# An expert stage with its maxima spread over the turn, its stacks copied by VectorE and its opening's loads in another order

## The reference

```python
def _expert(x, Wqkv, bqkv, Wo, bo, g1, be1, W1, bf1, W2, bf2, g2, be2):   # D=128, H=8 heads of 16, F=512
    qkv = x @ Wqkv.T + bqkv
    q, k, v = jnp.split(qkv, 3, axis=-1)
    q, k, v = (to_heads(q), to_heads(k), to_heads(v))
    attn = jax.nn.softmax(jnp.einsum('bhqd,bhkd->bhqk', q * scale, k), axis=-1)
    ctx = jnp.einsum('bhqk,bhkd->bhqd', attn, v).transpose(0, 2, 1, 3).reshape(b, s, d)
    ctx = ctx @ Wo.T + bo
    x = _layernorm(x + ctx, g1, be1)
    h = jax.nn.gelu(x @ W1.T + bf1, approximate=False)
    h = jax.nn.gelu(h @ W2.T + bf2, approximate=False)
    return _layernorm(x + h, g2, be2)
...
gated = probs * mask            # mask: the two largest of the softmax over 8 experts
gated = gated / (gated.sum(-1, keepdims=True) + 1e-09)
eo = jax.vmap(_expert, ...)(x, Wqkv, ...)
return jnp.einsum('ebsd,bse->bsd', eo, gated)
```

## Time and profile before

| | |
|---|---|
| median of 3 runs | 3488.11 us (3484.39 to 3490.66) |
| the profiled execution: own time, span | 3486.16 us, 3484.2 us |
| busy: PE, DVE, ACT, POOL | 81%, 50%, 56%, 16% |
| mean granted clock of TensorE | 0.91 of full speed |
| DMA | 304.09 MB, mean 87 GB/s |

### The profile page before, as it was taken

One profiled execution on the slowest core, in us unless ns is written; L12 is line 12 of the kernel. 1 busy time (PEld: TensorE's weight loads), 2 busy tenths in 40 slices (PEclk: granted clock), 3 DMA queues, 4 the chain that ended last, 5 costly groups with the idle time before them and its releaser, 6 DMA issues.

```text
span 3484.2 us, 66887 instructions
## 1 busy us (share of the span) xinstructions
PE 2811.9 (81%) x24695; PEld 1992.3 (57%) x24695; DVE 1737.3 (50%) x4806; ACT 1954.3 (56%) x4370; POOL 549.5 (16%) x732
## 2 busy tenths in 40 slices
PE   6778765888887888788887883778888969887898
PEld 5456443666665666566555561355565656555676
DVE  4665663555555555555555542234435453444454
ACT  2233223777776777677666664748435734773443
POOL 2000003333234322433212112000000000000000
PEclk9887876999999999999999986889979989998998
DMA  5000017565465655565445421010000000000000
GB/s 195 0 28 10 1 41 249 150 200 166 155 193 183 207 177 177 166 202 160 144 150 150 136 84 54 1 41 1 1 13 10 1 13 5 1 1 13 5 1 5
DMA packets 162579, 304.09 MB, mean 87 GB/s; under 512 B 19841, under 2 KB 121338, under 8 KB 154554
## 3 DMA queue, kind: packets, MB, share of 16 engines
q1 hardware_dynamic: 158930, 293.69, 27.0%
q0 software_dynamic: 3328, 6.14, 0.6%
HBM read 227.00 MB, written 72.75 MB: 86 GB/s over the span
## 4 chain that ended last, share of the span: by engine, by line
PE 48%; DVE 16%; ACT 11%; issue 11%; DVEq 5%; POOLq 3%; POOL 2%; PEld 1%; DMA 1%; SPq 1%; PEldq 1%; ACTq 0%
PE ps L1515 5%; PE ps L1832 5%; PE ps L1476 4%; PE ps L1497 3%; DVE peaks L2640 3%; PE ps L1313 3%; PE ps L1964 2%; PE ps L1764 2%; PE ps L1540 2%; ACT pt L2143 2%; PE ps L1902 2%; PE ps L1926 2%; PE ps L1549 2%; DVEq L2643 1%; PE ps L1298 1%
## 5 line engine op out<-in xcount | busy, mean ns | idle before, releaser
L2640 DVE TENSOR_REDUCE peaks<-ps 128x1 f32<-128x748 f32 x608 | 555.8, 933 | 557.5 <-PE ps L1476 548.4
L2143 ACT ACTIVATE pt<-ps 128x384 f32<-128x384 f32 x1216 | 570.9, 495 | 241.5 <-PE ps L1497 225.5
L1497 PE MATMUL ps<-qst,kst 98*128 98x128 bf16 x3648 | 403.0, 225 | 30.3 <-ACT pt L2143 10.1
L1497 PEld LDWEIGHTS ps<-qst,kst 98*128 98x128 bf16 x3648 | 271.9, 100 | 192.9 <-ACT pt L2143 62.2
L1133 POOL TENSOR_TENSOR rstd<-var,minus_half 128x6 f32<-128x6 f32 x40 | 53.0, 1324 | 1725.7 <-DVE var L2887 1278.9
L1476 PE MATMUL ps<-kst,qst 96*128 96x374 bf16 x1216 | 311.8, 339 | 11.0 <-DVE peaks L2640 11.0
L1515 PE MATMUL ps<-pt,vst 128*32 128x128 f32 (+1 forms) x7296 | 284.3, 287 | 0.0
L1515 PEld LDWEIGHTS ps<-pt,vst 128*32 128x32 f32 (+1 forms) x7296 | 199.5, 114 | 52.2 <-issue 26.0
L1484 PE MATMUL ps<-identb,peaks 128*2 128x128 bf16 x608 | 60.9, 225 | 82.6 <-DVE peaks L2646 66.6
L2163 ACT ACTIVATE qst<-ps 2x512 bf16<-2x512 f32 x152 | 89.7, 590 | 58.6 <-PE ps L1484 56.3
L1476 PEld LDWEIGHTS ps<-kst,qst 96*128 96x128 bf16 x1216 | 99.9, 102 | 22.7 <-DVE peaks L2640 19.2
(11 more groups left out here) (653 smaller groups left out, 6628.4 us busy)
## 6 DMA issues: line engine op xcount, KB each, us to landing
kst<-saved_k SPq DMA_DIRECT2D x76, 1176.0 KB
wf<-in_l SPq DMA_DIRECT2D x76, 512.0 KB, 5.6
saved_k<-kparts SPq DMA_DIRECT2D x168, 192.0 KB
vst<-saved_v SPq DMA_DIRECT2D x76, 408.0 KB, 4.9
saved_v<-vprod SPq DMA_DIRECT2D x32, 408.0 KB, 2.6
rows<-in_l_rows SPq DMA_DIRECT2D x76, 128.0 KB, 6.4
slots_x<-zeros SPq DMA_DIRECT2D x4, 1216.0 KB, 11.2
wq<-in_l SPq DMA_DIRECT2D x76, 64.0 KB, 4.1
```

What stands on the lines that cost most here:

```text
L1497: mm = pe.matmul(out[:, c * P:(c + 1) * P], kst[0:STACK + SHIFT, m % 3, head, j * P:(j + 1) * P], qst[0:STACK + SHIFT, m % 3, head, :], st ...
L2143: act.activation(pt[:, u % (2 * GROUP), :], entry()[:, 0:H0], ACT.Exp, scale=float(HD) ** -0.5)\
L2640: v.tensor_reduce(peaks[:, g, head:head + 1], entry()[:, :, 0:T // 2], XY, ALU.max)\
```

## The change

- Peaks stand at places 0, 2, 4 and so on to 14 instead of 0, 1, 3, 4, 6, 8, 10, 11. In burst turns the last four stay at place 9.
- The shift of group 0 moves from place 7 to 10, that of group 1 from place 14 of the turn before to place 4 of the tile's own turn.
- `query` moves from place 2 to 3, `out` from 10 to 11, `norm1` from 13 to 14, `turn_x1` from place 15 of turn n+1 to place 1 of turn n+2.
- `stack` becomes one step at place 7: eight products into a pair of banks and one VectorE copy of 96x1024, instead of two steps at 7 and 8 on the ring with ScalarE's copies.
- The opening loads `xb` first, then the key and value weights of all eight experts in one DMA into the room of `wf`, then the tables. `rank` (TensorE's part of the routing) comes before the keys instead of behind the second expert's. GpSimd splits the keys of three experts instead of four. The x tiles 0 to 2 are loaded at the end of the opening; the first burst's `wf` and rows at place 7 of turn 0.
- The semaphore `k_saved` becomes two, one for even and one for odd experts.

The diff:

```diff
@@ -233,7 +233,7 @@
-POOL_SPLITS = 4
+POOL_SPLITS = 3
@@ -274,20 +274,17 @@
 def opening_steps():
...
+    yield "load_xb", 0
+    yield "load_wkv_all",
...
-    yield "load_xb", 0
...
-    yield "load_wkv", 0, 0
+    yield "rank",
...
-        if e + 1 < E:
-            yield "load_wkv", 0, e + 1
...
-        if e == 1:
-            yield "rank",
@@ -295,9 +292,8 @@
-    yield "load_x", 0
-    yield "load_ffn", 0
-    yield "load_rows", 0
+    for m in range(3):
+        yield "load_x", m
@@ -309,30 +305,29 @@
-    if 0 <= n + 3 < RUN:
+    if 3 <= n + 3 < RUN:
...
-        put(2, ("query", early))
-        put(7, ("stack", early, 0))
-        put(8, ("stack", early, 1))
+        put(3, ("query", early))
+        put(7, ("stack", early))
...
-        for i, u in enumerate((0, 1, 3, 4)):
-            put(u, ("peak", following, i))
-        put(7, ("shift", following, 0))
-        put(14, ("shift", following, 1))
+        for i in range(GROUP):
+            put(2 * i, ("peak", following, i))
+        put(10, ("shift", following, 0))
...
-            for step, u in zip(late, (6, 8, 10, 11)):
+            for step, u in zip(late, (8, 10, 12, 14)):
...
+        put(4, ("shift", n, 1))
@@ -342,9 +337,10 @@
-        put(10, ("out", done))
-        put(13, ("norm1", done))
-        put(15, ("turn_x1", done))
+        put(11, ("out", done))
+        put(14, ("norm1", done))
+    if 0 <= n - 2 < RUN:
+        put(1, ("turn_x1", n - 2))
@@ -358,6 +354,8 @@
+    if n == 0:
+        put(7, ("load_ffn", 0), ("load_rows", 0))
@@ -399,9 +397,9 @@
-ENTRIES = {"scores": 1, "stack": 1, "biases": 1, "shift": 1, "turn_x": 1, "query": 1, "keys": 1, "values": 1, "turn_att": 1, "turn_x1": 1,
+ENTRIES = {"scores": 1, "biases": 1, "shift": 1, "turn_x": 1, "query": 1, "keys": 1, "values": 1, "turn_att": 1, "turn_x1": 1,
...
-PAIRS = {"peak": 1, "divide": 1, "out": 1, "back": 1}
+PAIRS = {"stack": 1, "peak": 1, "divide": 1, "out": 1, "back": 1}
@@ -720,6 +718,7 @@
+        wkv_room = wf[:, :, :].rearrange("p i f -> p (i f)")[:, 0:E * 2 * P].rearrange("p (e n) -> p e n", e=E)
@@ -955,8 +954,8 @@
-                        sp.wait_ge(S["k_saved"], 96 * E * (b + 1))
...
+                            sp.wait_ge(S[f"k_saved{i}"], 96 * E // 2 * (b + 1))
@@ -996,8 +995,7 @@
                 def load_wkv(b, e):
-                    if b * E + e >= 2:
-                        sp.wait_ge(S["ring_done"], made["values", b * E + e - 2])
+                    sp.wait_ge(S["ring_done"], made["values", b * E + e - 2])
@@ -1007,7 +1005,7 @@
-                            .then_inc(S["k_saved"], 16)
+                            .then_inc(S[f"k_saved{e % 2}"], 16)
@@ -1057,6 +1055,8 @@
                     elif what == "load_rows_of":
...
+                    elif what == "load_wkv_all":
+                        sp.dma_start(wkv_room, A["l1"][:, :, W1_K:W1_O].rearrange("e p n -> p e n")).then_inc(S["wkv_loaded0"], 16)
@@ -1422,16 +1422,16 @@
-                def stack(m, half):
-                    if half == 0:
-                        pe.wait_ge(S["parts_ready"], n.take("parts_ready"))
-                    out = bank()
-                    for i in range(GROUP):
-                        mm = pe.matmul(out[0:STACK, i * P:(i + 1) * P],
-                                       qs[:, m % 2, GROUP * half + i, :, :].rearrange("p g d -> p (g d)"), identb[:, :],
+                def stack(m):
+                    pe.wait_ge(S["parts_ready"], n.take("parts_ready"))
+                    out = pair()
+                    for i in range(E):
+                        half, at = divmod(i, GROUP)
+                        mm = pe.matmul(out[0:STACK, half, at * P:(at + 1) * P],
+                                       qs[:, m % 2, i, :, :].rearrange("p g d -> p (g d)"), identb[:, :],
...
-                    mm.then_inc(S["ring_ready"], 1)
-                    made["stack", m] = n.now("ring_done")
+                    mm.then_inc(S["peak_ready"], 1)
+                    made["stack", m] = n.now("peak_done")
@@ -1445,17 +1445,20 @@
+                def wkv_of(b, e):
+                    return wkv[:, e % 2, :] if b else wkv_room[:, e, :]
+
                 def keys(b, e, half):
-                    if half == 0:
+                    if half == 0 and (b or e == 0):
...
-                    pe.matmul(bank()[:, 0:hi - lo], wkv[:, e % 2, 0:P], xb[:, lo:hi], start=True, stop=True)\
+                    pe.matmul(bank()[:, 0:hi - lo], wkv_of(b, e)[:, 0:P], xb[:, lo:hi], start=True, stop=True)\
...
                 def values(b, e, half):
...
-                        mm = pe.matmul(out[:, i * P:(i + 1) * P], tile_of(xb, 3 * half + i), wkv[:, e % 2, P:2 * P],
+                        mm = pe.matmul(out[:, i * P:(i + 1) * P], tile_of(xb, 3 * half + i), wkv_of(b, e)[:, P:2 * P],
@@ -1470,7 +1473,7 @@
                 def peak(m, i):
...
-                        pe.wait_ge(S["ring_done"], made["stack", m])
+                        pe.wait_ge(S["peak_done"], made["stack", m])
@@ -2121,10 +2124,12 @@
                 def keys(b, e, half):
...
+                    if half == 0 and b == 0 and e >= 2:
+                        act.wait_ge(S[f"k_saved{e % 2}"], 96 * (e // 2))
+                    if half == 0 and b and e == 0:
+                        act.wait_ge(S["k_saved0"], 96 * E // 2 * b)
...
-                        act.wait_ge(S["k_saved"], 96 * (b * E + e))
-                    elif half == 0 and e >= 2:
-                        act.wait_ge(S["k_saved"], 96 * (e - 1))
+                        act.wait_ge(S[f"k_saved{(e - 1) % 2}"], 96 * ((b * E + e - 1) // 2 + 1))
@@ -2162,11 +2167,6 @@
-                                       ACT.Copy).then_inc(S["ring_done"], 1)
-                    elif what == "stack":
-                        m, half = at
-                        act.activation(qst[0:STACK, m % 3, GROUP * half:GROUP * (half + 1), :],
-                                       entry()[0:STACK, 0:GROUP * P].rearrange("p (h t) -> p h t", h=GROUP),
@@ -2714,6 +2714,9 @@
                     elif what == "peak":
...
+                    elif what == "stack":
+                        v.tensor_copy(qst[0:STACK, at[0] % 3, :, :].rearrange("p (a h) t -> p a (h t)", a=2),
+                                      entry()[0:STACK, :, :]).then_inc(S["peak_done"], 1)
                     elif what == "divide":
...
                     elif what == "out":
```

4 lines of the change are left out of this document (2 added, 2 removed).

## The result

The changed kernel takes **3312.91 us** in the median of four runs (3312.79 to 3322.13) against 3486.25 for the kernel before beside it: ratio 0.9514, 95% interval 0.9486 to 0.9543, some 173 us less. Measured once more in a later comparison (expected: 3313) it took 3313.04 us in the median of five runs, ratio 0.9507 (0.9487 to 0.9526); a sixth run, with the clock at 0.72 of full speed in the mean and 3650.65 us, is left out. The forecast was 3384, its range 3342 to 3440. The direction held, the size did not: 104 us were forecast.

The account below looks back on a forecast made before the run. TensorE was taken as the bound, busy 81% of the span, with 229 us idle in the expert stage. Loop 87 plus opening 17 made 104 off 3486.2, leaving 3382; the runs' median, 1.9 higher, gave 3384, range 3342 to 3440.

Parts of the forecast that it names:

- stack and query: In each turn: moving the stack saves no engine time; the later query spends 2.1 us of slack before the stack.
- The charge: Stack waiting for GpSimd's parts after the later query: 0.4 us a plain turn, bounds 0 and 1.5.
- those 229 us: TensorE's idle time in the expert stage, taken as the most a new order can return in the loop.
- the table of waits: TensorE's listed waits: shift product 64.0 us, attention transposes 36.1, stacks 17.0, shift product for score copies 14.5.
- VectorE's copy: The stack's new 96x1024 copy on VectorE: 1.2 us, between 691 ns and 1.38 us.
- Places of maxima and shift products: In a plain turn, the shift product's 1.57 us wait and the attention transpose's 0.46 us wait go.
- Classes of turns: Loop gain per turn: plain 1.6 us, with keys 0.9, burst 0.3, behind bursts 1.2 or 2.0, gather 3; 87 total.
- Wo product and norm steps: Wo product's move neutral; norm transpose's move no gain in plain turns, 3 us credited in each of three gather turns.
- Opening: Before the loop: saves 7.5 us sooner, kst load 9.4 us more, first maximum's product near 582; 17 us.
- 1, the clock: Denser loop turns win back 15 to 30 us of low clock: 3360, or 3345 without stack waits; chance 0.2.
- 2, new waits: Tighter turns make TensorE wait for banks and parts, 42 us back: 3426, to 3460 with a weak opening; chance 0.25.
- 3 and 4: Slower if GpSimd's parts come late to the stack, 3513, chance 0.07; no change, savings moved to ScalarE's ring, 3485, chance 0.04.

Follow-up runs that it names:

- a_query: Changed kernel with the query back at place 2 instead of 3; 3322.85 us, ratio 0.9538.
- a_stack: Changed kernel with the stack back as two ring steps at places 7 and 8, copied by ScalarE; 3341.72 us, ratio 0.9603.
- b_stack: Kernel before with only the stack moved to one step, pair of banks and VectorE's copy; 3429.01 us, ratio 0.9847.
- b_sp: Kernel before with the stack's move and the new places of maxima and shift products, nothing else; 3319.84 us, ratio 0.9527.
- b_loop: Kernel before with all changes of the loop but its own opening kept; 3327.81 us, ratio 0.9553.
- b_out: Kernel before with only the wo product moved from place 10 to 11; 3465.27 us, ratio 0.9959.

## Why the prediction was wrong, point by point

**The step that failed: stack and query.** It was a charge of 0.4 us in 34 turns and 0.3 in 18, 19 us (a_query's expectation took it over all turns, 30), and the two copies off ScalarE were credited with nothing. Measured, moving the stack gives 0.7 us in every plain and burst turn at the full clock, 52 us alone and 29 in the end. That turn of sign, 48 to 71 us, is most or all of the 69 that the forecast lacked. Two errors in it:
- *The charge.* The stack's waits for GpSimd stayed at 17.0 us in all. I had estimated that the parts need 2.6 us behind the query and the work in between takes 2.7; in the plain turn after they need 2.35 and it takes 3.09. So the parts come 0.74 us ahead of the stack, and the old place of the query was no better.
- *Two copies close together.* I saw ScalarE at 10.94 of 16 us in a plain turn and took its relief to be worth little. A share of busy time doesn't tell what 1.17 us at one spot do to a ring of three banks: two copies in a row cost 26 us, the same two apart nothing, and with the stack's halves one place apart the second half and a score product behind it start 0.35 and 0.31 us late (a_stack).

**The premise under it.** "The most a new order can return is those 229 us" was wrong, and so was reading the table of waits as all the waiting. Busy time is not a constant of the matmuls: 1234 before, 1195 after, 1220 in a_stack and 1191 in b_stack for the same 15740 or so, since waits of up to some 0.2 us lie inside it. In the turns of the earlier trace rows at the full clock it fell from 12.95 to 12.61 (plain) and from 20.76 to 20.50 (burst); over all classes I estimate 17 us. The rest of the 39, some 22, I put down to the clock.

**VectorE's copy**: 1.2 us taken, 1.22 measured: right. In the loop the products of the maxima wait 1.5 us in 3 places for it. By the cycle table of the Trainium skill ("VectorE: DVE Perf Modes", The TRN2 errata) the estimate was 1.19 for this copy and 1.14 for two of ScalarE's; the traces agree within 3%, with 1.22 and twice 0.583. Its line that VectorE sits closer to SBUF and ScalarE closer to PSUM (Specifications) says nothing on which queue has room, and that decided here.

**Places of maxima and shift products**: 1.57 + 0.46 = 2.03 forecast, 2.07 and 1.98 measured in plain turns at the full clock: right. Over the whole kernel my terms for the loop, 87 with the charge, stand against 128 for places alone, 109 beside the stack (b_stack to b_sp) and 38 with everything else in: with the low stretches of the clock, and with the wo product's move taking part of the same stall, there is no single price.

**Classes of turns**, sums before and after: 22 plain 64.6 us gained (forecast 35), 11 with keys 8.5 (11), 18 bursts 16.1 (5), behind bursts 30.0 and 29.9 (27 together), gather turns 20.6 (9), but the three merge turns behind these lost 13.2 (0), so that together the six gained 7.4: five or six of the twelve gathers now start in them, two before. Plain turns alone hold 30 of the miss. A clean one is 3.17 us shorter: 2.03 named, 0.7 of the stack, and some 0.4 of small waits that I left standing.

**Wo product and norm steps**: "neutral" was wrong: the wo product alone gains 14 us with the old places, and the three moves lose 13 with the new ones, where the transpose stands at place 1 behind a norm step that VectorE reaches late.

**Opening**: 17 forecast, 16.4 in the trace, 15 between b_loop and the changed kernel. The last key save starts at 568.60 (forecast 566.7), kst is issued at 575.91, 10.6 us sooner (forecast 12.7), and the first maximum's product comes at 584.47 (582). The size is right, the last step of the path is not: I let the load of kst gate that product, but it waited 1.19 us for the new copy on VectorE. Behind that lie the load of xg (transpose at 576.15, 6.34 us of wait), the query, and a stack at 581.98 that waited 3.46 us for GpSimd.

**Rivals.** 1, the clock: by the granted clock of the records, stretches at the lower level (1.2 GHz) within the loop fell from 142 to 77 us. I estimate its worth at some 22 us, what is left of the fall in busy time, inside the 15 to 30 of that rival; it was part of the truth. How much of it the dense turns caused was not shown: b_out, idle as before (224 us), had 87 us of low clock in its profiled run. 2, new waits: they came (61 us for xg and the norm step) but not in the ring, and did not take half: the norm step's share was 16.2 us before. 3 and 4 are refuted.

## What to carry to other kernels

Price an engine's work by its place, not by its share: two copies close together on the engine that frees a small ring can cost what they would not cost apart, and it is cheap to try them apart before giving them to another engine. Don't cap a gain by TensorE's idle time: compare the starts of its products, since a wait of 0.2 us leaves none. Edits that take the same stall don't add up: measure each from both ends, and compare turns at the same clock before explaining a difference. And look for what the denser schedule wants sooner: the loads issued one turn ahead were late here by up to 3.9 us.
